# Expert rows scaled by their gate and added onto x2 in DRAM by the scatter itself

## What is computed

```python
logits = x @ Wg + bg                                  # x is "x2" in the kernel, 64 experts
vals, idx = jax.lax.top_k(logits, TOP_K)              # TOP_K = 2
gates = jax.nn.softmax(vals, axis=-1)
...
slot = jnp.where(valid, e_s * CAP + rank, E * CAP)    # CAP = 1024 rows per expert, later ones are dropped
h1 = jax.nn.gelu(jnp.einsum('ecd,edh->ech', h, w1) + b1[:, None, :], approximate=False)
h2 = jnp.einsum('ech,ehd->ecd', h1, w2) + b2[:, None, :]
core = jnp.zeros((N, D), x.dtype).at[tok_s].add(g_s[:, None] * y_s)
...
y = x + core
mean = jnp.mean(y, axis=0)
var = jnp.mean((y - mean) ** 2, axis=0)
return (y - mean) * jax.lax.rsqrt(var + BN_EPS) * gamma + beta
```

## Time and profile before

| what | us |
|---|---|
| median of three runs (2711.33 to 2750.27) | 2736.12 |
| span of the profiled execution | 2422.4 |
| expert blocks, 1815 to 2244 us of the span | 429 |
| routing, 1640 to 1792 | 152 |
| mean, 2244 to 2318 | 74 |
| variance and output, 2318 to 2422 | 104 |

### The profile page before, as it was taken

The page is one execution under the profiler, slowest core; times in us unless marked ns, Lnnn a source line. Parts: engine busy times, 40 slices in busy tenths (PEclk is TensorE's granted clock), DMA queues, the critical chain, the costliest instruction groups (busy, mean ns, idle before and its releaser), DMA issues.

```text
span 2422.4 us, 50506 instructions
## 1 busy us (share of the span) xinstructions
PE 1978.3 (82%) x15238; PEld 1741.2 (72%) x15238; DVE 1451.4 (60%) x3750; ACT 409.5 (17%) x1197; POOL 1536.4 (63%) x1509
## 2 busy tenths in 40 slices
PE   2899999999997645999999999968628999999550
PEld 1788888888986534888889898857517778777240
DVE  6977777777874496566565655316723333333878
ACT  0211121212110243000000000004302222222030
POOL 5777776767777665777777777764754444444723
PEclk9999999999998887999999999969859999999675
DMA  5444343434436105333333333352128865668513
GB/s 170 121 125 118 118 121 115 122 100 121 123 94 203 38 20 165 112 114 107 112 109 104 106 107 105 105 185 60 48 71 265 250 196 158 189 206 264 171 43 106
DMA packets 219949, 312.93 MB, mean 129 GB/s; under 512 B 46946, under 2 KB 165017, under 8 KB 219788
## 3 DMA queue, kind: packets, MB, share of 16 engines
q0 software_dynamic: 61648, 155.25, 21.9%
q1 hardware_dynamic: 103148, 102.08, 13.0%
q10 hardware_dynamic: 54992, 53.49, 7.4%
HBM read 298.22 MB, written 57.83 MB: 147 GB/s over the span
## 4 chain that ended last, share of the span: by engine, by line
PE 49%; DVE 16%; issue 14%; DMA 8%; POOL 7%; DVEq 5%; SPq 1%; POOLq 0%; ACT 0%; ACTq 0%
PE bank L992 14%; PE bank L1022 13%; DMA acc<-x_scratch,acc 5%; POOL gath L670 4%; PE bank L1222 4%; PE bank L1213 4%; PE bank L1039 3%; DVE oh_lo L1354 3%; PE bank L1043 3%; PE bank L1114 2%; DVE codes L1376 2%; DVEq L1383 2%; PE bank L1056 2%; DVE oh_hi L1354 2%; DVEq L1407 2%
## 5 line engine op out<-in xcount | busy, mean ns | idle before, releaser
L670 POOL DMA_INDIRECT gath<-in_x_dram,idx_t x512 | 566.3, 1106 | 227.2 <-issue 129.6
L670 POOL DMA_INDIRECT gath<-h_scratch,idx_t x512 | 529.7, 1035 | 192.6 <-issue 139.8
L992 PE MATMUL bank<-onehot,gath 128*128 128x128 f32 x4096 | 522.0, 286 | 30.0 <-DMA gath<-h_scratch,idx_t 23.2
L1022 PE MATMUL bank<-Y,X 128*128 128x128 f32 x4312 | 534.6, 277 | 0.0
L1022 PEld LDWEIGHTS bank<-Y,X 128*128 128x128 f32 x4312 | 519.6, 193 | 15.4 <-issue 0.9
L992 PEld LDWEIGHTS bank<-onehot,gath 128*128 128x128 f32 x4096 | 494.8, 200 | 41.3 <-DMA gath<-h_scratch,idx_t 30.8
L1354 DVE TENSOR_TENSOR oh_lo<-iota_lo,lohi_t 128x512 bf16<-128x512 bf16 x392 | 268.4, 685 | 69.3 <-PE bank L1004 50.2
L1388 DVE TENSOR_TENSOR acc<-acc,bank 128x256 f32 x256 | 107.2, 419 | 282.3 <-issue 264.0
L763 POOL DMA_INDIRECT y_scratch<-acc x96 | 97.1, 1012 | 208.7 <-DVE acc L1755 203.1
L1039 PE MATMUL bank<-codes,oh_lo 128*128 128x400 bf16 x408 | 140.9, 346 | 107.4 <-DVE oh_hi L1354 48.0
L1222 PE MATMUL bank<-acc 128*128 128x256 f32 x768 | 198.7, 381 | 4.0 <-issue 3.8
(11 more groups left out here) (224 smaller groups left out, 2323.3 us busy)
## 6 DMA issues: line engine op xcount, KB each, us to landing
acc<-in_L_gnn_w_dram SPq DMA_DIRECT2D x101, 512.0 KB
acc<-in_L_gnn_w_dram ACTq DMA_DIRECT2D x96, 512.0 KB
y_scratch<-zero_s ACTq DMA_DIRECT2D x49, 256.0 KB
y_scratch<-bias_s SPq DMA_DIRECT2D x98, 128.0 KB
Y<-y_scratch SPq DMA_DIRECT2D x14, 896.0 KB, 12.9
acc<-in_L_gnn_b_dram ACTq DMA_DIRECT2D x96, 128.0 KB
gath<-in_x_dram,idx_t POOLq DMA_INDIRECT x512, 2.9
gath<-h_scratch,idx_t POOLq DMA_INDIRECT x512, 2.8
```

The costliest lines, as they stand in the source:

```text
L670: pool.indirect_dma_start(out=gath[:, half, k, :], out_offset=None, in_=table, in_offset=bass.IndirectOffsetOnAxis(ap=idx_t[:, TD + t:TD + ...
L992: last = pe.matmul(WINB[half][:, (q * DC + c) * WIN:(q * DC + c + 1) * WIN], gath[:, half, k, c * P:(c + 1) * P], onehot[:, half, k, :], s ...
L1022: last = pe.matmul(DB[w % 2][:, c * P:(c + 1) * P], X[:, h, c * P:(c + 1) * P], panel[:, w % 2, h, :], start=(h == 0), stop=(h == NT - 1))
```

## The change

- The slot table has two 4-byte words per slot: the token's number and the gate's value. Both are scattered by the same 98 DMAs, 8 bytes per row. The gate is computed per group in `place`: the difference of the two top logits (`gap`) by DVE, its exponential (`odds`) by ACT, then three chained DVE steps. `vals_t` and the softmax behind the last group are gone.
- `y_d` has one row per token and starts as a copy of x2: SP stores each x2 tile a second time. The 49 clearing DMAs are gone. Behind the 49 tiles lie 128 spare rows; the empty slots of a block are sent there, one row per partition, where before they were skipped.
- `row_ids` is one DVE step instead of three.
- DVE multiplies b2 by the gate (`b2g_s`) and the last step of a block is PSUM x gate + b2g.
- The scatter adds onto the rows in DRAM (`compute_op=ALU.add`). Since a token's two rows may meet, a scatter is issued only when the one before has landed (`yo_stored[1 - b]`). In each pair of blocks this wait stands on POOL ahead of the scatter.
- The mean's stage loads one row per token into `Y`. PE waits for the loads directly; DVE has no adds there. A group of seven tiles is loaded when PE has summed the group two before.

```diff
-    YROWS = 2 * NT * P
+    YROWS = (NT + 1) * P
...
-    slot_d = nc.dram_tensor("slot_scratch", (SLOTS + P, 1), I32).ap()
+    slot_d = nc.dram_tensor("slot_scratch", (SLOTS + P, 2), I32).ap()
...
-                    sp.dma_start(x2_d[ds(P * i, P), :], Y[:, ds(i, 1), :].rearrange("p a d -> p (a d)")
-                                 ).then_inc(x2_stored, 16)
+                    for d, stored in ((x2_d, x2_stored), (y_d, y_begun)):
+                        sp.dma_start(d[ds(P * i, P), :], Y[:, ds(i, 1), :].rearrange("p a d -> p (a d)")
+                                     ).then_inc(stored, 16)
...
-            def load_y(_, tiles):
-                for first, n, rows, k in parts(tiles):
-                    i = tiles[first]
-                    wait_count(sp, yb_added, i + n - SEVEN)
-                    for y_s, row in ((ya_s, P * i), (yb_s, N + P * i)):
-                        sp.dma_start(y_s[0:rows, first:first + n, :], tile_rows(y_d, row, n, rows)
-                                     ).then_inc(y_full[k], 16)
-            in_sevens(sp, NT, load_y)
+            for g in range(NG7):
+                wait_count(sp, mean_mm, SEVEN * (g - 1))
+                for first, n, rows, k in parts(range(SEVEN * g, SEVEN * (g + 1))):
+                    i = SEVEN * g + first
+                    sp.dma_start(Y[0:rows, i:i + n, :], tile_rows(y_d, P * i, n, rows)).then_inc(y_full[g % 2][k], 16)
...
                     spaced_wait(pool, yo_ready, blk + 1)
+                    spaced_wait(pool, yo_stored[1 - b], 16 * (j + b))
                     pool.indirect_dma_start(
                         out=y_d, in_=yo_s[:, b, :], in_offset=None,
                         out_offset=bass.IndirectOffsetOnAxis(ap=bids_s[:, b:b + 1], axis=0),
-                        bounds_check=ASSIGN - 1, oob_is_err=False).then_inc(yo_stored[b], 16)
+                        compute_op=ALU.add).then_inc(yo_stored[b], 16)
...
-                    act.dma_start(y_d[2 * P * st:2 * P * (st + 1), :].rearrange("(p r) d -> p r d", p=P),
-                                  zero_s[:, :].unsqueeze(1).to_broadcast([P, 2, D])).then_inc(y_cleared, 16)
...
+                v.tensor_tensor(gap[:, half, :], top8[:, :, 1], top8[:, :, 0], ALU.subtract).then_inc(gap_ready, 1)
...
-                v.tensor_copy(ids_s[:, half, :, :], ids_t[:, ds(G * g, G), :]).then_inc(route_step, 1)
-                step(g, 13, v.tensor_tensor(slot_s[:, half, :, :].rearrange("p t k -> p (t k)"), slotf, overf,
-                                            ALU.add))
+                for k in range(2):
+                    last = v.tensor_copy(entry_s[:, half, :, k, 0], ids_t[:, ds(G * g, G)])
+                last.then_inc(route_step, 1)
+                v.tensor_tensor(slot_s[:, half, :, :].rearrange("p t k -> p (t k)"), slotf, overf, ALU.add)
+                spaced_wait(dve, odds_ready, g + 1)
+                step(g, 13, v.tensor_scalar(den, odds[:, half, :], 1.0, None, ALU.add))
+                step(g, 14, v.reciprocal(entry_f[:, half, :, 0, 1], den))
+                step(g, 15, v.tensor_tensor(entry_f[:, half, :, 1, 1], odds[:, half, :], entry_f[:, half, :, 0, 1],
+                                            ALU.mult))
...
+                    spaced_wait(dve, w2_full[b], 32 * (j + 1))
+                    gate = gates_all[:, ds(blk, 1), 1:2].rearrange("p a e -> p (a e)")
+                    v.tensor_scalar(b2g_s[:, b, :], b2_s[:, b, :], gate, None, ALU.mult).then_inc(b2g_ready, 1)
                     spaced_wait(dve, yo_stored[b], 16 * j)
-                    v.tensor_copy(bids_s[:, b:b + 1], bids_all[:, ds(blk, 1)])
+                    v.tensor_scalar(bids_s[:, b:b + 1], bids_all[:, ds(blk, 1), 0:1].rearrange("p a e -> p (a e)"),
+                                    pad_row[:, 0:1], None, ALU.min)
+                    spaced_wait(dve, b2g_ready, blk + 1)
                     dve.wait_ge(mm2_done, blk + 1)
-                    v.tensor_tensor(yo_s[:, b, :], banks[6 + b][:, 0:D], b2_s[:, b, :], ALU.add
-                                    ).then_inc(yo_ready, 1)
+                    v.scalar_tensor_tensor(yo_s[:, b, :], banks[6 + b][:, 0:D], gate, b2g_s[:, b, :],
+                                           ALU.mult, ALU.add).then_inc(yo_ready, 1)
```

More of the change, by code:

```diff
@@ L765, in blocks @@
                         out_offset=bass.IndirectOffsetOnAxis(ap=bids_s[:, b:b + 1], axis=0),
-                        bounds_check=ASSIGN - 1, oob_is_err=False).then_inc(yo_stored[b], 16)
-            with pool.Fori(0, pairs) as j:
+                        compute_op=ALU.add).then_inc(yo_stored[b], 16)
+            blocks(0)
+            with pool.Fori(1, pairs) as j:
                 blocks(j)
@@ L905, in keep_x2, with odds_of, keep_route @@
                 stage_sums([i for i in ahead if not isinstance(i, int) or i < NT])
+            def odds_of(g, half):
+                spaced_wait(act, gap_ready, g + 1)
+                act.activation(odds[:, half, :], gap[:, half, :], ACT.Exp).then_inc(odds_ready, 1)
+            def keep_route(s, groups):
+                n = G * len(groups)
+                for q in range(0, n, 2):
+                    if q == 4 and not (isinstance(s, int) and s == 0):
+                        odds_of(2 * s - 1, 1)
+                    if q == G + 5:
+                        odds_of(2 * s, 0)
+                    keep_x2([2 * G * s + t for t in (q, q + 1) if t < n])
+                if len(groups) == 1:
+                    odds_of(2 * s, 0)
             act.wait_ge(sums_final, 2)
@@ L908, in _ @@
             stage_sums([2, 3])
-            keep_x2([0, 1])
-            with act.Fori(1, NT // 2 - 2) as j:
-                keep_x2([2 * j, 2 * j + 1])
-            for j in (NT // 2 - 2, NT // 2 - 1):
-                keep_x2([2 * j, 2 * j + 1])
-            keep_x2([NT - 1])
-            act.wait_ge(rsqrt_asked, 2)
-            act.activation(vals_t[:, :, 1:2], vals_t[:, :, 1:2], ACT.Exp).then_inc(sqrt_done, 1)
+            in_pairs(act, NG7, keep_route)
             act.wait_ge(blocks_ready, 1)
@@ L1241, in _, with col_sum, sums_sq @@
                 experts(j)
-            def col_sums(bank, data, ready, done):
-                def body(_, tiles):
-                    for b, i in enumerate(tiles):
-                        rows = LAST if isinstance(i, int) and i == NT - 1 else P
-                        pe.wait_ge(ready, i + 1)
-                        pe.matmul(bank[:, 0:D], ones_f[0:rows, :], data(b, i)[0:rows, :],
-                                  start=isinstance(i, int) and i == 0, stop=isinstance(i, int) and i == NT - 1
-                                  ).then_inc(done, 1)
-                return body
-            in_sevens(pe, NT, col_sums(banks[0], lambda b, i: Y[:, ds(i, 1), :].rearrange("p a d -> p (a d)"),
-                                       yb_added, mean_mm))
-            in_sevens(pe, NT, col_sums(banks[1], lambda b, i: sq_s[:, b, :], sq_ready, var_mm))
+            def col_sum(bank, data, i, done):
+                rows = LAST if isinstance(i, int) and i == NT - 1 else P
+                pe.matmul(bank[:, 0:D], ones_f[0:rows, :], data[0:rows, :],
+                          start=isinstance(i, int) and i == 0, stop=isinstance(i, int) and i == NT - 1
+                          ).then_inc(done, 1)
+            for g in range(NG7):
+                for first, n, _, k in parts(range(SEVEN * g, SEVEN * (g + 1))):
+                    pe.wait_ge(y_full[g % 2][k], 16 * (g // 2 + 1 if k < 3 else 1))
+                    for i in range(SEVEN * g + first, SEVEN * g + first + n):
+                        col_sum(banks[0], Y[:, i, :], i, mean_mm)
+            def sums_sq(_, tiles):
+                for b, i in enumerate(tiles):
+                    pe.wait_ge(sq_ready, i + 1)
+                    col_sum(banks[1], sq_s[:, b, :], i, var_mm)
+            in_sevens(pe, NT, sums_sq)
         @block.vector
@@ L1766, in _ @@
                 blocks(j)
-            def add_experts(group, tiles):
-                for first, n, _, k in parts(tiles):
-                    dve.wait_ge(y_full[k], 32 * (group + 1 if k < 3 else 1))
-                    for which, y_s, before_it, done in ((0, ya_s, None, ya_added), (1, yb_s, ya_added, yb_added)):
-                        for b in range(first, first + n):
-                            i = tiles[b]
-                            yi = Y[:, ds(i, 1), :].rearrange("p a d -> p (a d)")
-                            if before_it:
-                                dve.wait_ge(before_it, i + 1)
-                            v.scalar_tensor_tensor(yi, y_s[:, b, :],
-                                                   vals_t[:, ds(i, 1), which:which + 1].rearrange("p a b -> p (a b)"),
-                                                   yi, ALU.mult, ALU.add).then_inc(done, 1)
-            in_sevens(dve, NT, add_experts)
             dve.wait_ge(mean_mm, NT)
@@ L1820, in _ @@
             dve.wait_ge(stats2, NT)
-            row_norm(5)
+            row_norm(4)
```

91 lines of the change are left out of this document (39 added, 52 removed).

## The result

| | before | after |
|---|---|---|
| 20 runs each, median us | 2726.64 (2694.78 to 2753.84) | 2743.61 (2713.22 to 2759.96) |
| ratio | | 1.0068, 95% interval 1.0038 to 1.0098 |
| span of the profiled execution | | 2724.0 |

The account below looks back on a forecast made before the run. PE was taken to bound graph layers and quiet loop blocks, waits for gathered rows the busy ones. Routing +4, small steps -0.4, loop +42, mean -33 gave +13 on 2736.12: 2749 us, 8-in-10 range 2705 to 2890.

Parts of the forecast that it names:

- The base: Whole run: span 2422.4 us, median 2736.12; the 313.7 us outside the span were left as they are.
- The accumulating scatter and its wait: Expert loop: each scatter waits for the last one's landing, 5.4 us busy, 3.8 quiet; +31, +8 and +3, together +42.
- quiet blocks beyond 4.3 us: Sign of a wrong forecast in the loop: a landing exceeds PE's pace without traffic, and the loop costs over 100.
- well over 1.01 us: Sign of a wrong forecast in the loop: the accumulating scatter's issue takes well over 1.01 us.
- Landing becomes the loop's bound: Rival, chance 0.37: in the expert loop L is 7.7 us, busy blocks take 7.8; +150 in all, 2886 us.
- The lower bound of the range, 2705: Low end of the 8-in-10 range: the rival of a wholly hidden wait (chance 0.17, 2719 us) with the best mean.
- Mean: Mean stage: DVE's 98 adds and half the loads go; -33 us (-25 if the clock stays low, -39 at best).
- within 42: Sign of a right forecast: the mean is done within 42 us of the last scatter.
- Routing: Routing stage: extra DVE steps delay the first three groups; +4 us (0 with DVE slack, 8 if the exponential is late).
- Clearing y: Graph layers: 49 DMAs of ACT go where PE is the busy engine; 0 us, at best a few.
- three small steps: Expert loop: three small DVE steps less per block; only the first block gains, some 0.4 us.
- b2 times gate: Expert loop on DVE: last step 0.2 to 0.3 us later; about 10 us in busy places, counted within the loop's sum.

Follow-up runs that it names:

- p_wait_only: Kernel before with empty slots written to spare rows, plus only each plain scatter's wait for the one before: 2463.76 us, ratio 1.0127.
- h_two_halves_plain: Changed kernel with even and odd blocks scattering to two arrays, no wait for the neighbouring scatter, and scatters that overwrite instead of adding: 2417.88 us, ratio 0.9949.
- p_acc_only: Kernel before with empty slots written to spare rows, plus only the accumulating scatter, without the wait: 2471.88 us, ratio 1.0163.
- h_two_halves: Changed kernel with even blocks adding onto x2, odd ones onto a second cleared array, no wait for the neighbouring scatter: 2468.68 us, ratio 1.0162.
- p_acc_and_wait: Kernel before with empty slots written to spare rows, plus both accumulating scatter and wait for the one before: 2542.92 us, ratio 1.0452.
- a_whole_again: The unaltered changed kernel on a quick chip, against the kernel before on the same chip: 2483.57 us against 2429.44, ratio 1.0219.

## Why the prediction came out, step by step

- **The base: wrong.** "313.7 us lie outside the span, I leave them as they are". Nothing but 1.8 us lies outside. The difference of two chips was taken for a constant, and an effect sized on a quick chip (loop 428.5) was laid on the median of a slow one. On the quick chip the effect is +60.9 in the span, 1.0219 in the ratio. On the slow chip of the forecast the loop before has no trace; from 2743.61 - 2726.64 = +17 and the mean's -39 its loop should be some 56 us shorter than 529, near 473, as an estimate.
- **The accumulating scatter and its wait: the sum had +42, the loop took +101.0.** Between the same scatters as in the earlier trace rows, by their start times:

| blocks | us a block before | after | added | sum had |
|---|---|---|---|---|
| 44 where weights are loaded (0 to 32, 83 to 95) | 4.70 | 5.94 | 54 | 31 |
| 19 of the middle stretch (55 to 74) | 4.60 | 5.65 | 20 | 8 |
| 32 quiet ones (32 to 55, 74 to 83) | 4.19 | 5.02 | 27 | 3 |

  The step that failed is "a block can now be no shorter than the time L from a scatter's issue to its landing". The landings themselves came out near: 3.8 in quiet where the sum had "halfway, 3.8", which is luck, since it was the middle of bounds of 2.4 and 5.2, and a median of 5.0 where weights are loaded where it had 5.4. But the next scatter starts 0.85 us behind the landing, and this term was put at nothing. With it the quiet pitch is 4.65, over PE's 4.09, so "hidden" was wrong; without it the landing of 3.8 would have been hidden. A row for the term was there: in the earlier trace rows DVE's last step ends at 1981.99 and the scatter that waits for it starts at 1982.93, 0.94 later. As an estimate, 0.85 more a block in the prediction's own sum gives 45 x 1.55 + 19 x 1.25 + 32 x 0.53 = +110. The text had named the sign, "quiet blocks beyond 4.3 us", with "the loop costs over 100", but gave a landing longer than PE's pace as its reason, and that isn't what the landings show. An issue "well over 1.01 us" was the second sign, and it is 1.58.
- **Why the total came out even so: luck.** On a quick chip the same working would have been wrong by 41 us, +13 against 54.1. On a slow one the kernel before has a longer loop, 467.5 us instead of 428.5 on the chip of 2816, so that the change costs 61 there instead of 101 (56 by the estimate above on the chip of the forecast). This took away most of what the left-out term costs; a mean and a routing that came out some 10 us better than forecast took away the rest.
- **The rivals.** "Landing becomes the loop's bound" is what happened, 86 of 96 scatters, but at L = 4.4 in the median (7.1 at most) and not at 7.7, so with +101 instead of +179. A landing costs as soon as it and its 0.85 us pass a block's pace: in quiet blocks from 3.2 us on. The lower bound of the range, 2705, doesn't come out of its own terms: 12 + 4 - 39 = -23 gives 2713. The wait is not hidden even for a plain scatter (p_wait_only), so the rule of fixed 2.0 us plus bytes over 436 GB/s (the Trainium skill, DMA: Bandwidth & Descriptors, Anatomy of one DMA), 2.3 us here, holds for plain landings in quiet places (p_wait_only from 1982 to 2120: 2.4 at best, 2.5 in the median), and not for the median of all its plain ones, 3.9, nor for the quickest adding one, 3.6.
- **Mean: right.** -33 forecast, -39 at best; measured -39.9 on the quick chip. PE starts at 2351.58 after 8.3 us of idle time; the granted clock is 0.52 from 2352 to 2355, near the level of 1.2 GHz, and 1.00, that of 2.4 GHz, from 2355 on. So it did start low and rose. The stage ends 32.8 us behind the last scatter; "within 42" held.
- **Routing: right within its range.** +4 forecast, 0 found: the third group starts at 1696.82 on the quick chip, where the earlier trace rows had 1697.69, and the first scatter of the loop comes 0.3 us earlier.
- **Clearing y, three small steps, b2 times gate:** nothing or a few us. The loop starts 0.3 us earlier, and h_two_halves_plain leaves some 4 us for what was added to DVE in the loop.

The timeline at the mean of the quick run:

```profile
2344.93 1.58 POOL L762 DMA_INDIRECT y_scratch<-acc  x1 [2.98 <-issue]
2345.96 33.72 POOL L775 TENSOR_TENSOR X<-X,beta_s 128x256 f32<-128x256 f32 x49
2348.86 23.06 SPq L623 DMA_DIRECT2D Y<-y_scratch  x22
...
2377.69 0.42 DVE L1779 TENSOR_SCALAR acc<-bank 128x256 f32<-128x256 f32 x1 [33.78 <-PE bank L1249]
```

## What to carry to other kernels

A transfer that each block must wait out sets a pitch of its own: the time to its landing, and what goes by from there to the next issue, here 0.85 us. Compare that pitch with the pace of the engine that bounds the quiet blocks, not only with that of the busy ones: half a microsecond over it is paid in every block, and two costs that are each half hidden add up to more than their sum. Before an effect is laid on a time, make sure that trace and time come from the same chip: a span that is far shorter than the time is a sign that they don't.

## What the runs showed that I had not expected

- **An engine that adds on its own can be shut out for 27 us.** In p_acc_only POOL's 49 additions of beta begin 3 us ahead of the first load that DVE waits for, and DVE's first addition then takes 27.25 us. The groups of 2287 to 2320:

```profile
L780 POOL TENSOR_TENSOR X<-X,zero_s 128x256 f32 (+1 forms) x49 | 33.6, 1137 | 0.0
L1785 DVE SCALAR_TENSOR_TENSOR Y<-acc,vals_t,Y 128x256 f32<-128x256 f32 x1 | 27.2, 27250 | 8.6 <-DMA acc<-y_scratch 8.6
```

  In h_two_halves_plain the same two kinds run side by side at 0.74 and 0.84 us each, in h_two_halves DVE is shut out again, and the end stage takes 184.0 us instead of the 160.9 of the plain run: some 23 us that are no part of the scatter's landing. The Trainium skill, SBUF — State Buffer (Who interferes with whom), says that a vector instruction with two inputs in SBUF contends with a GpSimd instruction that reads SBUF, as an exclusive lock; the trace agrees, and shows beyond it that the loser may not get in between 30 or more instructions of the other. It happened in all three runs that have both additions and whose scatter adds (27.25, 27.53 and 27.39 us, p_acc_and_wait and h_two_halves being the others), and in none of the five in which the scatter overwrites, where DVE's longest took 0.95. Why this decides whether they alternate was not found. The changed kernel has no such addition on DVE, and its POOL needs 33.7 us instead of 40.95 in the same place.
- **From a scatter's landing to the start of the next that waits for it 0.85 us go by**, in seven traces (0.82 to 0.99), whether the scatter adds or overwrites; in a chain of such waits it belongs to each step.
- **An accumulating scatter of 128 rows costs GpSimd 1.58 us instead of 0.99** and lands in 3.6/4.4/7.1 us (a_whole_again) instead of 2.4/3.9/6.3 (p_wait_only), with 96 packets more for the same bytes.
- **Chips differ by 16% on one program** (2429 to 2816 us for the kernel before, in the median); a loop bound by a DMA's landing took 526.6 to 529.5 us on all of them.
